# Four weight buffers in place of two in the 512-wide mixtures of experts

## The reference

```python
def _L1_ffn_ref(x, gate, W1, b1, W2, b2):
    N_EXPERTS = 16
    TOP_K = int(N_EXPERTS * 0.2)
    raw_gate = jax.nn.softmax(jnp.einsum('btd,de->bte', x, gate), axis=-1)
    _, topk_idx = jax.lax.top_k(raw_gate, TOP_K)
    mask = jax.nn.one_hot(topk_idx, raw_gate.shape[-1], dtype=raw_gate.dtype).sum(axis=2)
    gate_topk = mask * raw_gate
    gate_topk = gate_topk / jnp.maximum(jnp.sum(jnp.abs(gate_topk), axis=-1, keepdims=True), EPS)
    hidden = jax.nn.relu(jnp.einsum('btd,edh->bteh', x, W1) + b1)
    expert_out = jnp.einsum('bteh,ehd->bted', hidden, W2) + b2
    return jnp.einsum('bte,bted->btd', gate_topk, expert_out)
```

## Time and profile before

| | us |
|---|---|
| three timed runs | 1794.38, 1800.07, 1803.42 |
| their median | 1800.07 |
| the profiled execution | 1793.91 |
| its span, first to last instruction | 1792.1 |
| TensorE busy, matmuls | 1510.6 (84%) |
| VectorE busy | 926.3 (52%) |
| ScalarE busy | 726.1 (41%) |
| GpSimd busy | 526.1 (29%) |
| mean granted clock of TensorE | 0.926 |

### The profile page before, as it was taken

The page is one execution under the profiler, slowest core; times in us unless marked ns, Lnnn a source line. Parts: engine busy times, 40 slices in busy tenths (PEclk is TensorE's granted clock), DMA queues, the critical chain, the costliest instruction groups (busy, mean ns, idle before and its releaser), DMA issues. The chain is left out here.

```text
span 1792.1 us, 44545 instructions
## 1 busy us (share of the span) xinstructions
PE 1510.6 (84%) x17326; PEld 1277.1 (71%) x17326; DVE 926.3 (52%) x2126; ACT 726.1 (41%) x1698; POOL 526.1 (29%) x771
## 2 busy tenths in 40 slices
PE   6999755899996999867799969998769988988884
PEld 5888644589994777755688857997558775766773
DVE  5666557631116888736522146665565444556313
ACT  3555456433342555433133325665222332544122
POOL 3444244122212443232244413221110210441341
PEclk9999886999998999988899989999889989988997
DMA  4111001188863111021599962332100566220785
GB/s 149 51 50 51 6 17 35 55 311 326 323 250 119 50 50 50 15 56 52 174 314 322 313 234 76 94 93 60 48 4 17 177 228 189 77 51 29 237 310 190
DMA packets 107000, 235.36 MB, mean 131 GB/s; under 512 B 36584, under 2 KB 56552, under 8 KB 99664
## 3 DMA queue, kind: packets, MB, share of 16 engines
q1 hardware_dynamic: 95040, 207.41, 35.9%
q0 software_dynamic: 8016, 21.90, 3.2%
q10 hardware_dynamic: 3776, 3.67, 0.6%
HBM read 213.07 MB, written 19.79 MB: 130 GB/s over the span
## 5 line engine op out<-in xcount | busy, mean ns | idle before, releaser
L2440 PEld LDWEIGHTS ps<-xt,w 128*128 128x128 f32 x1728 | 202.0, 192 | 38.2 <-issue 28.0
L2440 PE MATMUL ps<-xt,w 128*128 128x128 f32 x1728 | 211.4, 278 | 19.7 <-DMA w<-in_L_ffn_w 17.2
L2499 ACT ACTIVATE g<-ps,b 128x128 f32<-128x128 f32 x340 | 123.4, 367 | 239.8 <-PE ps L2440 197.8
L2450 PE MATMUL ps<-w,g 128*128 128x256 f32 x864 | 201.4, 380 | 1.1 <-issue 0.5
L2450 PEld LDWEIGHTS ps<-w,g 128*128 128x128 f32 x864 | 157.4, 190 | 20.1 <-issue 1.2
L2540 POOL DMA_INDIRECT results<-y,dest x85 | 84.1, 989 | 245.6 <-DVE y L2671 245.3
L2568 DVE COPY xt<-ps 128x256 f32<-128x256 f32 x85 | 36.1, 425 | 201.8 <-PE ps L2430 179.2
L2535 POOL DMA_INDIRECT x<-rows,token x82 | 80.1, 977 | 176.7 <-DVEq L2642 152.6
L2671 DVE COPY y<-ps 128x256 f32<-128x256 f32 x85 | 36.0, 424 | 151.5 <-PE ps L2450 151.5
L797 PE MATMUL ps<-c,w 128*128 128x258 f32 x512 | 93.7, 295 | 8.3 <-DVE pt L1108 6.7
L937 ACT ACTIVATE p<-sc,nmax 128x257 f32<-128x257 f32 x128 | 58.0, 503 | 81.2 <-DVE nmax L1065 81.2
(11 more groups left out here) (505 smaller groups left out, 3431.9 us busy)
## 6 DMA issues: line engine op xcount, KB each, us to landing
w<-in_L_ffn_w SPq DMA_DIRECT2D x124, 512.0 KB
w<-in_L_ffn_w SPq DMA_DIRECT2D x46, 1024.0 KB
c<-in_ctx SPq DMA_DIRECT2D x96, 258.0 KB, 2.8
w<-in_L_ffn_w SPq DMA_DIRECT2D x44, 256.0 KB, 3.9
rows<-in_w_L_xattn SPq DMA_DIRECT2D x32, 192.0 KB, 2.5
rows<-in_w_L_xattn SPq DMA_DIRECT2D x8, 768.0 KB
values<-v SPq DMA_DIRECT2D x8, 544.0 KB, 3.0
vx<-values SPq DMA_DIRECT2D x32, 136.0 KB, 3.5
```

The lines of the kernel that those rows point to most:

```text
L2440: mm = nc.tensor.matmul(hidden_bank(par, h), b.w1[:, par, c, h * P:(h + 1) * P], b.xt[:, par, c, :], start=c == 0, stop=c == DC - 1)
L2450: mm = nc.tensor.matmul(k.ps[:, YB + par, 0:D], b.g[:, par, h, :], b.w2[:, par, h, :], start=h == 0, stop=h == HC - 1)
L2499: nc.scalar.activation(b.g[:, par, h, :], hidden_bank(par, h), func, bias=b.b1[:, par, h:h + 1]).then_inc(s.g_ready, 1)
```

## The change

`mixture` gets a constant `RING`, which is 4 where the experts are 512 wide or less and 2 otherwise. `w1`, `b1` and `w2` get `RING` buffers with a semaphore each. SyncE loads the first `RING` blocks before its loop and then, at the same two waits as before, the weights of block n + `RING` in place of n + 2; the wait for the gathered rows stays in front of `w2` of block 1. SyncE's and ScalarE's loops hold `RING` blocks. TensorE's loop held four blocks already; it now takes its weights from buffer `slot % RING`. The buffers of `x`, `xt`, `g` and `y` and the accumulators are as before. With `RING` 2 the first mixture has the code of before, but for the unused semaphores. The names are made for all three.

```diff
--- before.py
+++ after.py
@@ -2323,8 +2323,9 @@
     NC = NB + NB % 2
     down = k.down8 if E == 8 else k.down16
     XB, HB, YB, IB = 0, 2, 6, 7
+    RING = 4 if hid <= 512 else 2
     names = ("logits_done rounded step exp_done mask_ready ranks_done z_kept first_ready hot_ready rows_done idx_ready experts_ready "
-             "w1_loaded0 w1_loaded1 b1_loaded0 b1_loaded1 w2_loaded0 w2_loaded1 x_loaded0 x_loaded1 x_loaded2 x_loaded3 comb_ready comb_turned comb_spread bias_done "
+             "w1_loaded0 w1_loaded1 w1_loaded2 w1_loaded3 b1_loaded0 b1_loaded1 b1_loaded2 b1_loaded3 w2_loaded0 w2_loaded1 w2_loaded2 w2_loaded3 x_loaded0 x_loaded1 x_loaded2 x_loaded3 comb_ready comb_turned comb_spread bias_done "
              "sent0 sent1 xt_done xt_ready h_done g_ready y_done y_ready summed noted squared rooted inverted scaled finished " + " ".join(f"back{t}" for t in range(NT)))
     with stage(k, names) as (block, s), \
             buffers(k, l=[P, NT, E], r=[P, NT, E], eq=[P, NT, E], pick=[P, top, NT, E], pr=[P, NT, E],
@@ -2335,11 +2336,13 @@
             buffers(k, square=[P, D], mean=[P, NT], root=[P, NT], inverse=[P, NT]) as fin, \
             buffers(k, F32R, mask=[P, NT, E], hot=[P, top, NT, P], ids=[P, top, NT, NC], ones=[P, P], before=[P, P]) as r_, \
             buffers(k, mybir.dt.int32, at=[P, top, NT], lo=[P, top, NT], dest=[P, NB], token=[P, NB], expert=[P, NB]) as u, \
-            buffers(k, w1=[P, 2, DC, hid], b1=[P, 2, HC], w2=[P, 2, HC, D], x=[P, 4, D], xt=[P, 2, DC, P],
+            buffers(k, w1=[P, RING, DC, hid], b1=[P, RING, HC], w2=[P, RING, HC, D], x=[P, 4, D], xt=[P, 2, DC, P],
                     g=[P, 2, HC, P], y=[P, 2, D], back=[P, NT, top, D]) as b, \
             (buffers(k, comb_t=[P, NT, P]) if b1 is not None else nullcontext(None)) as turned:
-        w1_loaded, w2_loaded = [s.w1_loaded0, s.w1_loaded1], [s.w2_loaded0, s.w2_loaded1]
-        b1_loaded, sent = [s.b1_loaded0, s.b1_loaded1], [s.sent0, s.sent1]
+        w1_loaded = [s.w1_loaded0, s.w1_loaded1, s.w1_loaded2, s.w1_loaded3]
+        w2_loaded = [s.w2_loaded0, s.w2_loaded1, s.w2_loaded2, s.w2_loaded3]
+        b1_loaded = [s.b1_loaded0, s.b1_loaded1, s.b1_loaded2, s.b1_loaded3]
+        sent = [s.sent0, s.sent1]
         x_loaded = [s.x_loaded0, s.x_loaded1, s.x_loaded2, s.x_loaded3]
         returned = [s.back0, s.back1, s.back2, s.back3, s.back4, s.back5, s.back6, s.back7]
 
@@ -2351,35 +2354,35 @@
 
         @block.sync
         def _(sp):
-            def load_w1(n, par):
+            def load_w1(n, at):
                 e = sp.value_load(u.expert[0:1, ds(n, 1)], min_val=0, max_val=n_exp - 1)
-                sp.dma_start(b.w1[:, par], w1[ds(e, 1)].rearrange("a p c n -> (a p) c n")).then_inc(w1_loaded[par], 16)
+                sp.dma_start(b.w1[:, at], w1[ds(e, 1)].rearrange("a p c n -> (a p) c n")).then_inc(w1_loaded[at], 16)
                 if b1 is not None:
-                    sp.dma_start(b.b1[:, par, :], b1[:, ds(e * HC, HC)]).then_inc(b1_loaded[par], 16)
+                    sp.dma_start(b.b1[:, at, :], b1[:, ds(e * HC, HC)]).then_inc(b1_loaded[at], 16)
                 return e
 
-            def load_w2(e, par):
-                sp.dma_start(b.w2[:, par], w2[ds(e, 1)].rearrange("a p h d -> (a p) h d")).then_inc(w2_loaded[par], 16)
-
-            def body(n, par):
+            def load_w2(e, at):
+                sp.dma_start(b.w2[:, at], w2[ds(e, 1)].rearrange("a p h d -> (a p) h d")).then_inc(w2_loaded[at], 16)
+
+            def body(n, at):
                 sp.wait_ge(s.g_ready, (n + 1) * HC)
-                e = load_w1(n + 2, par)
+                e = load_w1(n + RING, at)
                 sp.wait_ge(s.y_done, n + 1)
-                load_w2(e, par)
+                load_w2(e, at)
 
             sp.dma_start(k.rows.rearrange("(t p) d -> p t d", p=P), k.z[:]).then_inc(s.z_kept, 16)
             sp.wait_ge(s.experts_ready, 1)
-            for par in range(2):
-                e = load_w1(par, par)
-                if par == 1:
+            for at in range(RING):
+                e = load_w1(at, at)
+                if at == 1:
                     sp.wait_ge(x_loaded[1], 16)
-                load_w2(e, par)
+                load_w2(e, at)
             fetch_weights(k, sp)
-            with sp.Fori(0, (NB - 2) // 2) as it:
-                for par in range(2):
-                    body(2 * it + par, par)
-            for n in range((NB - 2) // 2 * 2, NB - 2):
-                body(n, n % 2)
+            with sp.Fori(0, (NB - RING) // RING) as it:
+                for at in range(RING):
+                    body(RING * it + at, at)
+            for n in range((NB - RING) // RING * RING, NB - RING):
+                body(n, n % RING)
             sp.wait_ge(sent[0], 16 * ((NB + 1) // 2))
             sp.wait_ge(sent[1], 16 * (NB // 2))
             for t in range(0, NT, 2):
@@ -2430,33 +2433,38 @@
                     mm = nc.tensor.transpose(k.ps[:, XB + slot % 2, c * P:(c + 1) * P], b.x[:, slot, c * P:(c + 1) * P], k.ident)
                 mm.then_inc(s.xt_done, 1)
 
-            def hidden(n, par, turns, first):
-                pe.wait_ge(w1_loaded[par], 16 * (turns + 1))
+            def place_of(slot, rounds):
+
+                return slot % RING, 4 // RING * rounds + slot // RING
+
+            def hidden(n, slot, rounds, first):
+                par, (at, turns) = slot % 2, place_of(slot, rounds)
+                pe.wait_ge(w1_loaded[at], 16 * (turns + 1))
                 pe.wait_ge(s.xt_ready, n + 1)
                 for h in range(HC):
                     if not first or par * HC + h >= 4:
                         pe.wait_ge(s.g_ready, n * HC + h - 3)
                     for c in range(DC):
-                        mm = nc.tensor.matmul(hidden_bank(par, h), b.w1[:, par, c, h * P:(h + 1) * P], b.xt[:, par, c, :],
+                        mm = nc.tensor.matmul(hidden_bank(par, h), b.w1[:, at, c, h * P:(h + 1) * P], b.xt[:, par, c, :],
                                               start=c == 0, stop=c == DC - 1)
                     mm.then_inc(s.h_done, 1)
 
-            def outputs(n, par, turns, first):
-                pe.wait_ge(w2_loaded[par], 16 * (turns + 1))
+            def outputs(n, slot, rounds, first):
+                par, (at, turns) = slot % 2, place_of(slot, rounds)
+                pe.wait_ge(w2_loaded[at], 16 * (turns + 1))
                 if not first:
                     pe.wait_ge(s.y_ready, n - 1)
                 for h in range(HC):
                     pe.wait_ge(s.g_ready, n * HC + h + 1)
-                    mm = nc.tensor.matmul(k.ps[:, YB + par, 0:D], b.g[:, par, h, :], b.w2[:, par, h, :],
+                    mm = nc.tensor.matmul(k.ps[:, YB + par, 0:D], b.g[:, par, h, :], b.w2[:, at, h, :],
                                           start=h == 0, stop=h == HC - 1)
                 mm.then_inc(s.y_done, 1)
 
             def body(n, slot, rounds, first=False, last=False):
-                par, turns = slot % 2, 2 * rounds + slot // 2
-                hidden(n, par, turns, first)
+                hidden(n, slot, rounds, first)
                 if not last:
                     turn(n + 1, (slot + 1) % 4, rounds + (slot + 1) // 4)
-                outputs(n, par, turns, first)
+                outputs(n, slot, rounds, first)
 
             def first_body():
                 hidden(0, 0, 0, True)
@@ -2490,14 +2498,15 @@
 
         @block.scalar
         def _(act):
-            def body(n, par, turns):
+            def body(n, at, turns):
+                par = at % 2
                 if b1 is not None:
-                    act.wait_ge(b1_loaded[par], 16 * (turns + 1))
+                    act.wait_ge(b1_loaded[at], 16 * (turns + 1))
                 for h in range(HC):
                     act.wait_ge(s.h_done, n * HC + h + 1)
                     if b1 is not None:
                         nc.scalar.activation(b.g[:, par, h, :], hidden_bank(par, h), func,
-                                             bias=b.b1[:, par, h:h + 1]).then_inc(s.g_ready, 1)
+                                             bias=b.b1[:, at, h:h + 1]).then_inc(s.g_ready, 1)
                     else:
                         nc.scalar.activation(b.g[:, par, h, :], hidden_bank(par, h), func).then_inc(s.g_ready, 1)
 
@@ -2507,11 +2516,11 @@
             nc.scalar.activation(f.pr[:], f.l[:] if kind == "capacity" else f.pr[:], ACT.Exp,
                                  scale=-1.0 if kind == "capacity" else 1.0).then_inc(s.exp_done, 1)
             nc.scalar.activation(f.warm[:], k.ones[:, 0:1], func)
-            with act.Fori(0, NB // 2) as it:
-                for par in range(2):
-                    body(2 * it + par, par, it)
-            if NB % 2:
-                body(NB - 1, 0, NB // 2)
+            with act.Fori(0, NB // RING) as it:
+                for at in range(RING):
+                    body(RING * it + at, at, it)
+            for n in range(NB // RING * RING, NB):
```

(2 more changed lines are left out.)

## The result

The changed kernel takes 1768.47 us in the median (1766.53 to 1780.79) beside 1798.35 us for the kernel before: a ratio of 0.9858, interval 0.9828 to 0.9889, about 25 us less with 20 to 31 as its bounds. The forecast was 15 us and 1785; the sign was right, the size was too small by ten microseconds, and 1768 lies under the range's low end of 1776.

The account below looks back on a forecast made before the run. The prediction took late weight loads as the present loss and the DMA engines as the next bound, close above TensorE. 15.3 us steady gain less 0.3 for small edits made 15 us off 1800.07: 1785, range 1776 to 1795.

Parts of the forecast that it names:

- The latency loop: 512-wide mixtures: block n+2 waits for a load issued at block n's hidden values; four buffers add at least 7.5 us.
- What a block costs the DMA engines: Steady blocks: 3.87 and 3.80 us of transfers at a full share, plus 0.06, so 3.93 and 3.86 us.
- TensorE's own work: Steady blocks without waits: 3.80 us a block in the second mixture, 3.73 us in the last.
- rival B: TensorE becomes the bound of both stages' blocks: gain 22.6 us, time 1777.5; chance 0.17.
- The sum: Steady part of both stages: 7.4 us gained in the second mixture, 7.9 in the last, together 15.3 us.
- The start of the stages: First blocks of each mixture: between 1 us gained from earlier loads and 2 us lost to delayed gathers; taken as 0.
- a gap that stays: Last mixture, in front of block 2: the late start, 6.76 us from block 1 to 2, was to remain.
- The small edits: Six more semaphores a mixture and longer SyncE and ScalarE loops: a cost of 0.3 us in all.
- C: Rival: the DMA stream is already at its ceiling, 4.07 us a block; gain 6.1 us, time 1794; chance 0.20.
- D: Rival: result writes starve behind queued weights and set the block; loss 32 us, time 1832; chance 0.03.
- E: Rival: SyncE reaches its two waits late, so loads don't come forward; no gain, time 1800; chance 0.03.
- The median: Whole kernel: the 15 us gain was taken off the timed runs' median of 1800.07 us, giving 1785.

Follow-up runs that it names:

- e3_two_ahead: Changed kernel with each later load issued two blocks later, so two blocks ahead; prologue still loads four blocks: 1787.37 us, ratio 0.9959 to the kernel before.
- e4_three_ahead: Changed kernel with each later load issued one block later, so three blocks ahead: 1768.07 us, ratio 0.9842 to the kernel before.
- e13_two_first: Kernel before's schedule (two blocks loaded in the prologue, later loads two ahead) with four buffers instead of two: 1796.58 us, ratio 1.0006.
- e6_extra_load: Changed kernel plus one unread 512 KB load a block in both 512-wide mixtures, which TensorE waits for: 1820.35 us.
- e12_two_extra: Two buffers as in the kernel before, plus one unread 512 KB load a block in both 512-wide mixtures: 1856.49 us.
- e11_two_small: Two buffers as in the kernel before, but weight loads past the first blocks move 64 bytes a partition instead of 4 KB: 1766.99 us.
- e8_again: The changed kernel run and profiled once more, nothing altered: 1770.68 us, ratio 0.9843 to the kernel before.

## Why the prediction was wrong

**The latency loop.** Right. Its waits went, "issue" waits among them, and the chain of the last mixture has one weight load left. e3_two_ahead and e4_three_ahead show where it breaks. In the changed kernel the transfers' view has the time from issue to landing (890 to 1010):

```profile
DMA packets 17544, 43.47 MB, mean 362 GB/s; under 512 B 6955, under 2 KB 6955, under 8 KB 17542
...
w<-in_L_ffn_w SPq DMA_DIRECT2D x65, 512.0 KB, 5.5
...
results<-y,dest POOLq DMA_INDIRECT x32, 5.6
```

A load lands 5.5 us after its issue here; with two blocks ahead it took 5.1 us in e13_two_first. Two blocks ahead leave about two blocks less the hidden part, some 5.5 us, at TensorE's pace, and between the hidden values and the landing SyncE also reads the expert and issues the load, 0.8 to 1.4 us where the chain shows it. Together that is more than 5.5; three blocks leave 9.2. One turn of the loop in the kernel before (the hidden values of block n are ready at 1702.7, its load of block n + 2 starts at 1704.10):

```profile
1700.60 1.35 PE ps L2440 x12
1702.02 0.41 issue
1702.82 0.69 SPq L2355
1704.10 6.05 DMA w<-in_L_ffn_w
1710.36 2.05 PE ps L2440 x16
```

No run takes SyncE's microsecond away by itself, so how much of the loss it was stays open.

**What a block costs the DMA engines.** This is the step that failed. I divided the rate by the share, 322 GB/s by 0.95 and 300 by 0.87, and took 339 and 345 GB/s for the engines' limit with this mix. With the engines' floor set at 3.87 and 3.80 us a block, and 0.06 added, the DMA engines became the bound in the forecast; TensorE, at 3.73, was. The changed kernel moved 351 GB/s at 0.98 and 366 at 1.01 with TensorE never waiting, 386 at 1.03 while it built up its lead, and e6_extra_load 401 at 1.03. The share counts the time that packets are under way, and with few of them asked for the same packets are under way for longer: e12_two_extra moves 13% less than e6_extra_load at a share only 0.05 lower, which comes to 0.123 us a packet and engine beside 0.113. The range of 3.67 to 4.07 us a block did not hold what the transfers of a block cost at these rates, 1.31 MB / 386 GB/s = 3.39 us, or 3.27 at the 401 of a kernel with more plain loads in its mix. I had the row that spoke against my choice, 357 GB/s in a deep queue, and set it aside because it held no gathers.

**TensorE's own work.** 3.80 us in the second mixture was too much. It is 3.73, as e11_two_small shows; neighbours 3.77 to 3.86 apart were not free of waits. With the two terms rival B would have given 36 x (4.136 - 3.73) + 10.5 = 25.1 us.

**The sum.** From block 2 to the last the second mixture gained (1035.11 - 886.20) - (1020.94 - 885.00) = 13.0 us where I had 7.4, and the last 85.09 - (1751.56 - 1675.07) = 8.6 where I had 7.9; 21.6 us for 15.3. These differences stop short of the whole gain, because block 3 comes late in this execution and block 2 does not. From block 3 on they are 35 x (4.144 - 3.735) = 14.3 and 19 x (4.276 - 3.737) = 10.2, together 24.6 of the stages' 25.1 us.

**The start of the stages.** I took 0, and that was right. From the start of the stage to block 2 it is 36.0 us before and 34.5 after in the second mixture, 39.5 and 37.7 in the last, 3.3 us less; but to block 3 it is 39.9 and 39.7, 43.3 and 43.2, only 0.3 us less. What I called a gap that stays moved on to block 3 in this execution, with 5.2 and 5.5 us; in e8_again block 2 comes just 0.3 and 0.7 us earlier than before. The prologue's lead is worth something where the loads behind it are late: 7 us in e3_two_ahead.

**The small edits.** Semaphores and longer loops cost nothing that shows: e13_two_first has them all, and 1.0006 with an interval of 3 us down and 5 us up, in which the 0.3 us that I took would not be seen.

**The rivals.** B was right in kind: blocks at 3.73 us and no waits for weights, but with a share of 0.98 to 1.01 and not 0.95. C fell with it: 322 GB/s was no ceiling. D did not happen. With the queue full a result lands 5.6 us after its issue in the median, where the last write took 2.4 us; but the weights' depth has little part in that, since with two blocks ahead it was 5.0 us in e13_two_first already, and 5.5 with three. In the last mixture's first blocks VectorE did wait for a write. In its waits over the whole span that is one line:

```profile
  DMA results<-y,dest: 4.5, 2
```

The copy that ended the longer of these waits began at 1680.44 us, and TensorE went on at 1680.55 for its weights' sake. Two blocks are 7.5 us, so the landing has 2 us to spare in the steady part. E fell with the result itself.

**The median.** The forecast set the gain off against 1800.07, and the runs of the kernel before had 1798.35 in the end. Of the 16.5 us between 1785 and 1768.47, 10.5 are the gain and 1.7 this; the other 4.3 lie between the ratio, which gives 1772.8, and a median of four runs. 1772.8 is under 1776 too. The clock is below 0.9 in 15 of the 40 slices, not 14; nothing rested on that.

## What to carry to other kernels

A DMA share near 1 is no proof that the transfers are the bound. Where the kernel keeps few loads under way, ask for the GB/s of the fullest queue in the same trace, and take as the engine's floor the smallest distance of blocks, not the middle one (in the second mixture 3.77 us, against a true 3.73). Prefetch depth is counted in time: a load has to be issued earlier than it takes to land under full traffic, here 5.5 us and about one more for the engine that issues it, and every load of the block has to be, or the wait moves to the one that is not; a fourth block of lead brought nothing here over three.

## What the runs showed of the hardware

The rate of the 16 DMA engines for loads of 4 KB a partition with gathers and writes beside them was 322 GB/s with two blocks of 1 MB of weights asked for and 386 with four, while the lead was built up, at shares of 0.95 and 1.03; with blocks of 1.5 MB it was 349 with two and 401 with four, at 0.98 and 1.03. The Trainium skill's page "DMA: Bandwidth & Descriptors" (section "Where 436 GB/s comes from") has about 358 GB/s as the HBM's share of a core, and says that it binds between HBM and SBUF; here a single core moved 401, so in these runs it did not bind, and that the row of 357 GB/s lay next to it was a coincidence. The page's table of measured loads (section "Bandwidth") has 425 GB/s for a core alone with large transfers, and 435 for the ports; the 401 lie below both.

In the second mixture, 890 to 1010, an indirect write of results landed 5.0 us after its issue with two blocks of weights asked for (e13_two_first), 5.5 with three (e4_three_ahead) and 5.6 with four, beside 2.4 us with little else under way. In the changed kernel's stretch 890 to 920 the weight loads took 8.1 us to land, and the writes still 5.7. So a write waits little for the weights that are queued. By the page's turn by turn between queue rows it would be so too: these runs agree with that rule, though they do not single it out.

Executions of the same instructions differed by 11 us in a single stretch of 600 us (granted clock 0.92 against 0.90), which is more than half of what this change was forecast to bring.
